# A post-norm transformer layer: first FFN layer as three fp32r products, one more FFN group ahead of the last output projection, the last group in two banks, later results on ScalarE

## The chip, the cores and the metric

One core of one Trainium2 chip runs the whole program. TensorE (PE) multiplies, VectorE (DVE), ScalarE (ACT) and GpSimd (POOL) do the elementwise work, SyncE (SP) starts the DMAs. The metric is device time in microseconds; before the change three runs took 1055.47 to 1058.67, median 1057.71.

## The reference

```python
# x: (4, 1024, 128), 16 heads of 64, all fp32
q, k, v = (einsum('BSE,EHK->BSHK', x, w) for w in (w_q, w_k, w_v))
probs = softmax(q @ k^T / sqrt(64) + causal_mask)
x = layernorm(x + einsum('BSHK,EHK->BSE', probs @ v, w_o))
h = x @ W_exp + b_exp                  # 128 -> 512
h = butterfly(h, up_weights)           # 9 linear stages
h = gelu(h + up_bias)
h = butterfly(h, down_weights)         # 9 linear stages
x = layernorm(x + h @ W_con + b_con + down_bias)
```

Both butterflies are linear, so the kernel composes them into the weights: `W1` (128 x 512) and `W2` (512 x 128). What runs over the 4096 tokens is attention, x1 = layernorm, `gelu(x1 @ W1 + b) @ W2`, and a layernorm.

## The kernel before

**Tiling.** The 4096 tokens are 32 tiles of 128 rows (`X`, batch b has 8 of them) or 8 groups of 512 (`TPC` = 4 tiles). Attention runs over 32 units, one for each batch and pair of heads. A unit has 12 steps (query chunk of 512, key tile of 128). Each step computes scores transposed, as two fp32r matmuls for each head (lines 671 and 675), exponentials on ScalarE (841), a mask (483) and a running sum of probabilities on GpSimd (498, 506, 507). `PV_AFTER` says behind which steps the value products stand (696): steps 0 to 6 of a unit behind its own steps 8 and 9, steps 7 to 11 behind step 1 of the next unit, or, for the last unit, behind everything (`PV_LEFT`).

**Order.** Every engine has its own instruction list, in an order written out by hand. `FILL`, `OUT_AT` and `X1_AT` place "fillers" for TensorE (projections 597 to 599, row maxima 621, output projection 636, transposes of x1 641, transposes of W2 645, sums 658) between the scores of a step (place 0), behind them (1) or behind the value products (2). The other engines walk the same lists (`evacuate` on ScalarE, `consume` on VectorE). Four PSUM banks `WORK` serve the fillers in turn; a filler waits until its bank's last reader is through. The score banks are `SC`, the value products' banks `O`.

**Softmax sums.** `norm` (651) multiplies the sums by ones when GpSimd's last addition of a unit is through. ScalarE writes them to `R0` (828), a DMA spreads them, VectorE takes the reciprocal (`recip`, 1027), two more DMAs copy it to all rows (`inverses`, 395), and `scale` (1032) multiplies `O` by it, after which the output projection and the next value products may use `OT` and `O`. In a unit, `recip` stands behind step 2 (`RECIP_AFTER`), `scale` behind step 6, in the last unit behind step 4 (`LAST_SCALE`).

**x1.** The first six groups (`EARLY_GROUPS`, batches 0 to 2) are normalised during later attention units, transposed by TensorE in steps 2, 3, 4, 9, 10 and 11 of the last unit, copied by VectorE into `x1T`, which lies in `WQKV` (1003), and get b_con + down_bias added in place (1015). Groups 6 and 7 follow after the last output projection: `transpose_x1` (733) and `copy_x1t` (1072).

**FFN.** `up(g)` (739) makes four hidden tiles of a group, one fp32 matmul of 128 x 512 each (746; the profile shows two instructions for each); `hid_banks` are `SC0`, `SC1` and two `WORK` banks, and a tile of group g waits for the Gelu of the same tile of group g - 1. ScalarE applies Gelu (876) into `G`, which has `DOWN_LAG` + 1 buffers. `down(g)` (749) makes the 16 products of a group (758, again two instructions each) into one of two `y_banks`. The order on TensorE is `PV_LEFT`, `norm`, `up(0)` to `up(2)`, the last output projection (636, two chunks of 16 instructions), and then `up(g)`, `down(g - 3)` in turn, with the transposes of groups 6 and 7 between, and three `down` at the end.

**End.** VectorE adds each group's product to X (`residual`: 1091, statistics 1095 and 1098), GpSimd makes (variance + eps)^-0.5 of it (`deviation`, 525: lines 528 and 531), VectorE normalises four tiles (`result`, 1100: line 1019), and SyncE stores the group (433).

Of the kernel before, what the change touches and what calls it, by code (L numbers as in the profile page):

```python
# [188 lines left out]
def post_norm_layer(nc, x, w_q, w_k, w_v, w_o, W_exp, b_exp, up_w, up_b, down_w, W_con, b_con, down_b, out):  # L189
    ctx = ExitStack()  # L190
    with ctx:
# [35 lines left out]
        RSTD = sb("RSTD", [P, B * TILES])  # L227
        HALF = sb("HALF", [P, B * TILES])
        W1 = sb("W1", [P, HID])
        SW = sb("SW", [P, 2 * HID])  # L230
# [19 lines left out]
        w2t = W2[:, :, :].rearrange("p t d -> p (t d)")  # L250
        x1T = [WQKV[:, g // 2, g % 2 * CH:(g % 2 + 1) * CH] for g in range(EARLY_GROUPS)]
        G = [w_raw[:, i * HT * CH:(i + 1) * HT * CH].rearrange("p (t c) -> p t c", t=HT) for i in range(DOWN_LAG + 1)]

# [31 lines left out]
        h1_added, stats_made = sem("h1_added"), sem("stats_made")  # L285
        x1_made, x1t_made, x1t_copied = sem("x1_made"), sem("x1t_made"), sem("x1t_copied")
        hid_ready, gelu_done, y_ready, h2_made = sem("hid_ready"), sem("gelu_done"), sem("y_ready"), sem("h2_made")
        out_made, out_stored = sem("out_made"), sem("out_stored")

# [56 lines left out]
        def _(sp):  # L346
# [83 lines left out]

            for g in range(B * CHUNKS):
                sp.wait_ge(out_made, (g + 1) * TPC)
                sp.dma_start(out_tiles[:, g * TPC:(g + 1) * TPC, :],
                             X[:, g * TPC:(g + 1) * TPC, :]).then_inc(out_stored, 16)
            sp.wait_ge(out_stored, 16 * B * CHUNKS)


        @block.gpsimd
        def _(pool):
# [108 lines left out]
            deviation((B - 1) * TILES, B * TILES)  # L548
            for g in range(B * CHUNKS):
                pool.wait_ge(x1_made, (g + 1) * TPC)  # L550
                pool.wait_ge(stats_made, (B * CHUNKS + g + 1) * TPC)
                deviation(g * TPC, (g + 1) * TPC)


        @block.tensor
        def _(pe):
# [181 lines left out]

            def up(g):
                pe.wait_ge(x1t_copied, g + 1)  # L740
                for t_ in range(HT):
                    if g == 0 and t_ >= 2:
                        evacuated(LAST_NORM - 3 + t_)
                    if g > 0:
                        pe.wait_ge(gelu_done, (g - 1) * HT + t_ + 1)
                    nc.tensor.matmul(hid_banks[t_], W1[:, t_ * P:(t_ + 1) * P], x1T[g % EARLY_GROUPS], start=True,  # L746
                                     stop=True).then_inc(hid_ready, 1)

            def down(g):
                pe.wait_ge(gelu_done, (g + 1) * HT)  # L750
                if g < 2:
                    evacuated(LAST_OUT + g)
                    evacuated(NUMBER[UNITS - 1, ("w2", 0)])
                else:
                    pe.wait_ge(h2_made, g - 1)
                for i in range(TPC):
                    for t_ in range(HT):
                        t = nc.tensor.matmul(y_banks[g % 2][:, i * P:(i + 1) * P], G[g % (DOWN_LAG + 1)][:, t_, i * P:(i + 1) * P],  # L758
                                             W2[:, t_, :], start=t_ == 0, stop=t_ == HT - 1)
                t.then_inc(y_ready, 1)  # L760

            for g in range(DOWN_LAG):
                up(g)
# [12 lines left out]
        def _(act):  # L776
# [25 lines left out]
            def evacuate(u, f, at):  # L802

                w, free = WORK[at % NWORK], work_free[at % NWORK]
                if f[0] in ("max", "mt", "out", "x1", "w2"):
                    return
                act.wait_ge(work_ready, at + 1)
                if f[0] == "proj":
                    _, n, c = f
                    nxt = (u + 1 + (f == EARLY)) % 2  # L810
                    cols = slice(c * CH, (c + 1) * CH)
                    T = QH if n == 0 else KHL
                    hi(T[0:K, nxt, 0, cols], w[0:K, :])
                    hi(T[K:P, nxt, 1, cols], w[K:P, :]).then_inc(qk_hi, 1)
                elif f[0] == "v":
                    unit, slots, tile = v_units(u)
                    if f[1] == 0 and u > 0:

                        act.wait_ge(pv_done, (u - u % 2) * NS + PV_CREDIT)
                    V = VHI if tile else VLO  # L820
                    dst = V[:, unit % slots:unit % slots + 2, 2 * f[1]:2 * f[1] + 2, :].rearrange("p u t k -> p t u k")
                    hi(dst, w[:, :].rearrange("p (t u k) -> p t u k", t=2, u=2)).then_inc(free, 1)
                elif f[0] == "lay":
                    lo = f[1] % 2 * S + f[2] * 2 * P
                    hi(XTH[:, lo:lo + 2 * P], w[:, 0:2 * P]).then_inc(xt_hi, 1)
                else:
                    act.wait_ge(sums_landed, (u - 1) * 16 + 16)
                    nc.scalar.activation(R0[:, :], w[:, :], ACT.Copy).then_inc(sums_out, 1)
                    act.wait_ge(sums_out, u)
                    act.sem_inc(free, 1)  # L830
# [40 lines left out]
            for g in range(B * CHUNKS):  # L871
                for t_ in range(HT):
                    act.wait_ge(hid_ready, g * HT + t_ + 1)
                    if t_ == 0 and g > DOWN_LAG:
                        act.wait_ge(y_ready, g - DOWN_LAG)
                    nc.scalar.activation(G[g % (DOWN_LAG + 1)][:, t_, :], hid_banks[t_], ACT.Gelu,
                                         bias=BIAS1[:, t_:t_ + 1]).then_inc(gelu_done, 1)

        @block.vector
        def _(dve):  # L880
# [54 lines left out]
            def consume(u, f, at):  # L935
# [136 lines left out]
            def copy_x1t(g):  # L1072

                dve.wait_ge(x1t_made, g - EARLY_GROUPS + 1)
                dve.wait_ge(hid_ready, (g - EARLY_GROUPS + 1) * HT)
                nc.vector.tensor_copy(x1T[g % EARLY_GROUPS], O[g % 2][:, :]).then_inc(x1t_copied, 1)
                add_bc(g)
# [8 lines left out]

            def residual(g):

                dve.wait_ge(y_ready, g + 1)
                xs = X[:, g * TPC:(g + 1) * TPC, :]  # L1090
                nc.vector.tensor_tensor(xs, y_banks[g % 2][:, :].rearrange("p (t d) -> p t d", t=TPC), xs,
                                        ALU.add).then_inc(h2_made, 1)
                dve.wait_ge(h2_made, g + 1)
                for i in range(TPC):
                    nc.vector.bn_stats(BS[:, i, :], X[:, g * TPC + i, :]).then_inc(h1_added, 1)
                dve.wait_ge(h1_added, (B * CHUNKS + g + 1) * TPC)
                for i in range(TPC):
                    nc.vector.bn_aggr(MV[:, g * TPC + i, :], BS[:, i, :]).then_inc(stats_made, 1)

            def result(g):  # L1100
                dve.wait_ge(rstd_made, B + g + 1)
                normalise(g, out_made)
# [4 lines left out]
            for g in range(B * CHUNKS):  # L1107
                residual(g)
                if g > 0:
                    result(g - 1)  # L1110
                if g + EARLY_GROUPS < B * CHUNKS:
                    copy_x1t(g + EARLY_GROUPS)
            result(B * CHUNKS - 1)


# [26 lines left out]
```

## Time and profile before

| | us |
|---|---|
| median of three runs | 1057.71 |
| profiled execution | 1057.07 |
| its span, first to last instruction | 1054.7 |
| TensorE busy | 1016.9 (96%) |
| GpSimd busy | 757.4 (72%) |
| VectorE busy | 754.2 (72%) |
| ScalarE busy | 602.9 (57%) |

The profile is of one execution of the program. Matmuls are pipelined: the duration of one holds the time until its result is out, so the pace is read from start to start. In the timelines a row is start, duration, engine, line, operation, output and inputs, count, and in brackets the idle time of the engine just before it and what ended it. In the chain of waits each piece released the next. "PEld" is TensorE's weight load, which runs beside the matmuls. The mean granted TensorE clock was 0.989 of full speed.

### The profile page before, as it was taken

How to read it: one execution, taken by the hardware profiler on the slowest of the kernel's cores; microseconds unless marked ns; L12 is line 12 of the kernel's file. 1: busy time of each engine (PE TensorE's matmuls, PEld its weight loads, DVE VectorE, ACT ScalarE, POOL GpSimd, SP SyncE). 2: the span in 40 equal slices, each digit the busy share in tenths (PEclk: the TensorE clock that was granted, in tenths of full speed). 3: DMA queues.
4: the chain of work that ended last, by engine and by line, in shares of the span. 5: the costliest groups of instructions: out<-in, count | busy, mean ns of one | idle time of the engine just before them, and what ended most of it. 6: DMA issues, size and time to landing. Idle time of an engine off the chain costs nothing.

```text
span 1054.7 us, 17699 instructions
## 1 busy us (share of the span) xinstructions
PE 1016.9 (96%) x5816; PEld 697.3 (66%) x5816; DVE 754.2 (72%) x2014; ACT 602.9 (57%) x1214; POOL 757.4 (72%) x726
## 2 busy tenths in 40 slices
PE   4799999999999999999999999999999999999997
PEld 3556666676666666767666766766666676675576
DVE  6666777777677778777778777776778778873456
ACT  4355566665565566666656556666656656664431
POOL 6278776777779777777779877777778987777322
PEclk9699999999999999999999999999999999999998
DMA  7112223232231223232231222332222222320002
GB/s 221 45 46 66 56 57 82 62 81 75 48 81 38 65 62 82 62 81 62 62 81 47 66 53 61 81 81 62 72 52 81 63 51 53 80 62 21 21 18 64
DMA packets 45800, 68.69 MB, mean 65 GB/s; under 512 B 15079, under 2 KB 21515, under 8 KB 45710
## 3 DMA queue, kind: packets, MB, share of 16 engines
q1 hardware_dynamic: 45710, 67.57, 25.2%
q8 instruction: 47, 0.77, 0.3%
q14 instruction: 43, 0.35, 0.1%
HBM read 31.11 MB, written 2.36 MB: 32 GB/s over the span
## 4 chain that ended last, share of the span: by engine, by line
PE 86%; DMA 6%; POOL 3%; DVE 2%; issue 2%; SPq 1%; ACT 0%; POOLq 0%; DVEq 0%; ACTq 0%
PE O L696 24%; PE WORK L621 13%; PE SC L671 12%; PE SC L675 12%; PE WORK L636 4%; PE WORK L658 3%; PE WORK L758 3%; PE WORK L599 3%; PE WORK L598 3%; PE WORK L597 3%; DMA QL<-NROW 2%; DMA R<-RROW 2%; PE SC L746 1%; PE WORK L746 1%; PE WORK L607 1%
## 5 line engine op out<-in xcount | busy, mean ns | idle before, releaser
L841 ACT ACTIVATE PR<-SC 128x512 f32<-128x512 f32 (+3 forms) x768 | 355.0, 490 | 283.4 <-PE SC L675 247.3
L498 POOL TENSOR_TENSOR SUM<-SUM,PR 128x1024 f32<-128x1024 f32 (+3 forms) x256 | 419.1, 1637 | 14.0
L966 DVE CUSTOM_DVE_ANT_0 WORK<-WORK,CMASK 128x128 f32<-128x128 f32 (+3 forms) x512 | 239.4, 514 | 65.0 <-PE WORK L621 65.0
L671 PE MATMUL SC<-QH,KHL 128*128 128x512 f32 (+3 forms) x768 | 272.0, 359 | 4.8 <-ACT PR L841 3.2
L675 PE MATMUL SC<-QL,KH 128*128 128x512 f32 (+3 forms) x768 | 263.9, 347 | 3.1 <-DMA QL<-NROW 3.0
L483 POOL TENSOR_SCALAR_AFFINE_SELECT PR<-PR 128x256 f32<-128x256 f32 x256 | 105.7, 414 | 213.1 <-ACT PR L841 212.9
L621 PE MATMUL WORK<-KHL,QH 128*128 128x512 f32 (+3 forms) x768 | 224.8, 361 | 5.1 <-DMA KH<-KHL 3.7
L696 PE MATMUL O<-PR,VLO 128*64 128x512 f32 (+3 forms) x1024 | 200.0, 522 | 2.0 <-DVE OT L1036 1.9
L671 PEld LDWEIGHTS SC<-QH,KHL 128*128 128x128 f32 x768 | 145.3, 189 | 63.3 <-ACT PR L841 29.2
L621 PEld LDWEIGHTS WORK<-KHL,QH 128*128 128x128 f32 x768 | 135.5, 190 | 55.8 <-issue 34.9
L969 DVE TENSOR_REDUCE MP<-WORK 128x1 f32<-128x512 f32 x256 | 164.3, 685 | 4.6
L675 PEld LDWEIGHTS SC<-QL,KH 128*128 128x128 f32 x768 | 145.5, 189 | 16.3 <-DMA QL<-NROW 5.9
L890 DVE TENSOR_TENSOR QL<-WORK,QH 64x512 fp32r<-64x512 f32 x128 | 88.1, 688 | 78.6 <-ACT QH L778 77.6
L507 POOL TENSOR_TENSOR SUM<-PR 128x768 f32<-128x768 f32 x64 | 136.3, 2130 | 1.4 <-ACT PR L841 1.4
L696 PEld LDWEIGHTS O<-PR,VLO 128*64 128x64 f32 x1024 | 64.9, 136 | 106.3 <-issue 78.4
L890 DVE TENSOR_TENSOR KHL<-WORK,KHL 64x512 fp32r<-64x512 f32 x128 | 88.1, 688 | 43.2 <-ACT KHL L778 41.1
L778 ACT ACTIVATE QH<-WORK 64x512 fp32r<-64x512 f32 x128 | 75.6, 590 | 28.6 <-PE WORK L599 27.8
L778 ACT ACTIVATE KHL<-WORK 64x512 fp32r<-64x512 f32 x128 | 75.9, 593 | 4.7 <-PE WORK L599 1.4
L696 PE MATMUL O<-PR,VHI 128*64 128x256 f32 (+3 forms) x512 | 74.3, 432 | 0.0
L966 DVE DVE_READ_ACCUMULATOR2_ANT MP<- 128x1 f32 x512 | 72.7, 142 | 0.0
L696 PEld LDWEIGHTS O<-PR,VHI 128*64 128x64 f32 x512 | 36.8, 137 | 52.6 <-issue 46.8
L636 PE MATMUL WORK<-WOT,OT 128*128 128x128 f32 x512 | 63.7, 278 | 0.0
(102 smaller groups left out, 1070.9 us busy)
## 6 DMA issues: line engine op xcount, KB each, us to landing
QH<-QH SPq DMA_DIRECT2D x128, 128.0 KB, 2.3
KH<-KHL SPq DMA_DIRECT2D x128, 128.0 KB, 2.3
R<-RROW SPq DMA_DIRECT2D x64, 256.0 KB, 3.9
SW<-in_L_ffn_up_weights_dram SPq DMA_DIRECT2D x9, 512.0 KB, 4.7
SW<-_L_ffn_down_weights_dram SPq DMA_DIRECT2D x9, 512.0 KB, 4.8
out_dram<-X SPq DMA_DIRECT2D x8, 256.0 KB, 2.3
QL<-NROW SPq DMA_DIRECT2D x64, 4.0 KB
X<-in_L_attn_x_BSE_dram SPq DMA_DIRECT2D x1, 512.0 KB, 4.3
```

Of the source, the lines that this page charges most:

```text
L498: nc.gpsimd.tensor_tensor(total, total, prob(unit, s), ALU.add).then_inc(add_done, 1)
L507: nc.gpsimd.tensor_tensor(total, first[:, :, START[s]:], prob(unit, s), ALU.add).then_inc(add_done, 1)
L621: t = nc.tensor.matmul(w[:, at_col:at_col + n], QH[:, nxt, h, qt * P:(qt + 1) * P], KHL[:, nxt, h, lo:lo + n], start=True, stop=True)
L636: t = nc.tensor.matmul(w[:, k * P:(k + 1) * P], attended(pair, qc)[:, k * P:(k + 1) * P], WOT[:, pair % PAIRS, :], start=pair < last, stop ...
L671: nc.tensor.matmul(dst, KHL[:, par, h, kt * P:(kt + 1) * P], QH[:, par, h, q0:q0 + n], start=True, stop=False)
L675: nc.tensor.matmul(dst, KH1[:, par, h, kt * P:(kt + 1) * P], QL[:, par, h, q0:q0 + n], start=False, stop=True).then_inc(scores_ready, 1)
L696: t = nc.tensor.matmul(O[qc][h * K:(h + 1) * K, START[s]:], values(unit, kt)[:, h * K:(h + 1) * K], p[:, h, :], start=kt == 0, stop=s == L ...
L778: return nc.scalar.activation(dst, src, ACT.Copy)
L841: nc.scalar.activation(prob(unit, s)[:, h, :], SC[use % NSC][:, 0:n], ACT.Exp, scale=K ** -0.5).then_inc(exp_done, 1)
L890: return nc.vector.tensor_tensor(dst, src, hi_part.bitcast(F32), ALU.subtract)
L966: op = nc.vector.tensor_tensor_reduce(cols, cols, CMASK[:, CH - n:], 1.0, LOWEST, ALU.add, ALU.max, cell)
L969: op = nc.vector.tensor_reduce(cell, cols, AX_X, ALU.max)
```

## The change

`DOWN_LAG` is 4: four groups of hidden tiles stand ahead of the last output projection, and the fifth buffer of `G` lies in `WQKV`. `W1` and x1 transposed are split into a high part, rounded to fp32r by ScalarE (`hi`), and a low part, the difference, by VectorE (`lo`); a hidden tile is three fp32r matmuls. The high parts of x1 lie in `QH` and `QL`, the low parts in `KHL` and `KH1`, the split W1 in `WST` and `WSV`, so that no group waits for another's buffer. W1 is split in step 8 of the last unit. The first two hidden tiles go ahead of the sums of the last unit. The last group is two pieces of two tiles, in two banks. Results of the first three pieces stay on VectorE, those of the other six go to ScalarE as x * rstd + shift, where GpSimd makes shift = -mean * rstd in two more operations. In the last unit `recip` and `scale` move up, to steps 1 and 3.

```diff
-DOWN_LAG = 3
+DOWN_LAG = 4
-LAST_SCALE = 4
+LAST_RECIP, LAST_SCALE = 1, 3
+FFN_PIECES = [(g * TPC, (g + 1) * TPC) for g in range(B * CHUNKS - 1)]
+FFN_PIECES += [(B * TILES - TPC, B * TILES - 2), (B * TILES - 2, B * TILES)]
+ACT_RESULTS = 3
+W1_SPLIT_AT = (UNITS - 1, 8)
...
+        def y_bank(tile):
+            return O[0] if tile >= FFN_PIECES[-1][0] else y_banks[tile // TPC % 2]
...   # SyncE: one store for each piece
+            for n, (first, end) in enumerate(FFN_PIECES):
+                if n < ACT_RESULTS:
+                    sp.wait_ge(out_made, end)
+                else:
+                    sp.wait_ge(act_out_made, end - FFN_PIECES[ACT_RESULTS][0])
+                sp.dma_start(out_tiles[:, first:end, :], X[:, first:end, :]).then_inc(out_stored, 16)
...   # GpSimd
+                deviation(first, end)
+                if n >= ACT_RESULTS:
+                    pool.wait_ge(rstd_made, B + n + 1)
+                    nc.gpsimd.tensor_tensor(SHIFT[:, first:end], MV[:, first:end, 0], RSTD[:, first:end],
+                                            ALU.mult).then_inc(shift_mult, 1)
+                    pool.wait_ge(shift_mult, n - ACT_RESULTS + 1)
+                    nc.gpsimd.tensor_scalar(SHIFT[:, first:end], SHIFT[:, first:end], -1.0, None,
+                                            ALU.mult).then_inc(shift_made, 1)
...   # TensorE
-            norm(take_work(LAST_NORM), UNITS - 1)
-            pe.wait_ge(exp_done, UNITS * 2 * NS + EXP_CREDIT)
-            def up(g):
+            def up(g, tiles=range(HT)):
                 pe.wait_ge(x1t_copied, g + 1)
-                for t_ in range(HT):
+                pe.wait_ge(w1_lo, 1)
+                for t_ in tiles:
...
-                    nc.tensor.matmul(hid_banks[t_], W1[:, t_ * P:(t_ + 1) * P], x1T[g % EARLY_GROUPS], start=True,
+                    rows = slice(t_ * P, (t_ + 1) * P)
+                    nc.tensor.matmul(hid_banks[t_], W1H[:, rows], x1_hi_slots[g], start=True, stop=False)
+                    nc.tensor.matmul(hid_banks[t_], W1L[:, rows], x1_hi_slots[g], start=False, stop=False)
+                    nc.tensor.matmul(hid_banks[t_], W1H[:, rows], x1_lo_slots[g], start=False,
                                      stop=True).then_inc(hid_ready, 1)
...
-            for g in range(DOWN_LAG):
+            pe.wait_ge(exp_done, UNITS * 2 * NS + EXP_CREDIT)
+            up(0, range(2))
+            norm(take_work(LAST_NORM), UNITS - 1)
+            up(0, range(2, HT))
+            for g in range(1, DOWN_LAG):
                 up(g)
...   # ScalarE
+                if f[0] == "x1":
+                    hi(x1_hi_slots[f[1]], w[:, :]).then_inc(x1t_hi, 1)
+                    return
...
+                    if (u, s) == W1_SPLIT_AT:
+                        act.wait_ge(composed, 3 * STAGES)
+                        hi(W1H, W1[:, :]).then_inc(w1_hi, 1)
...
+                n = g - (EARLY_GROUPS - 2)
+                if 0 <= n < B * CHUNKS - EARLY_GROUPS:
+                    act.wait_ge(x1t_made, n + 1)
+                    hi(x1_hi_slots[EARLY_GROUPS + n], O[(EARLY_GROUPS + n) % 2][:, :]).then_inc(x1t_hi, 1)
+            for n in range(ACT_RESULTS, len(FFN_PIECES)):
+                act.wait_ge(shift_made, n - ACT_RESULTS + 1)
+                for t in range(*FFN_PIECES[n]):
+                    nc.scalar.activation(X[:, t, :], X[:, t, :], ACT.Identity, scale=RSTD[:, t:t + 1],
+                                         bias=SHIFT[:, t:t + 1]).then_inc(act_out_made, 1)
...   # VectorE
-                    dve.wait_ge(work_ready, at + 1)
-                    nc.vector.tensor_copy(x1T[g], w[:, :]).then_inc(x1t_copied, 1)
+                    dve.wait_ge(x1t_hi, g + 1)
+                    lo(x1_lo_slots[g], w[:, :], x1_hi_slots[g]).then_inc(x1t_copied, 1)
...
+                    if (u, s) == W1_SPLIT_AT:
+                        dve.wait_ge(w1_hi, 1)
+                        lo(W1L, W1[:, :], W1H).then_inc(w1_lo, 1)
-                    if s == RECIP_AFTER and u > 0:
+                    if s == (RECIP_AFTER if u < UNITS - 1 else LAST_RECIP) and u > 0:
...
+            for n in range(len(FFN_PIECES)):
+                residual(n)
+                if 0 < n <= ACT_RESULTS:
+                    result(n - 1)
+                if n + EARLY_GROUPS < B * CHUNKS:
+                    copy_x1t(n + EARLY_GROUPS)
```

## Rows read from the trace of the kernel before

**Rows 1.** The page's chain that ended last, share of the span by engine

```profile
PE 86%; DMA 6%; POOL 3%; DVE 2%; issue 2%; SPq 1%; ACT 0%; POOLq 0%; DVEq 0%; ACTq 0%
```

**Rows 2.** Busy by stretch: stretch, us, PE, PEld, DVE, ACT, POOL, clock, DMA share, GB/s

```profile
962.83:985.24 22.41, 20.70 (x123) 12.41 (x122) 13.34 (x17) 8.07 (x18) 21.96 (x17) 1.00 0.09 25
985.38:1047.15 61.77, 61.76 (x368) 45.42 (x368) 29.64 (x120) 23.55 (x34) 11.45 (x16) 1.00 0.11 31
1047.15:1054.70 7.55, 0.00 (x0) 0.00 (x0) 4.06 (x17) 0.00 (x0) 1.50 (x3) 0.64 0.36 104
```

**Rows 3.** The chain in order of time, from the last sums: start, us, what

```profile
985.38 1.06 PE WORK L658 x8
...
988.35 1.72 PE WORK L746 x4
...
996.94 3.57 PE WORK L636 x32
...
1003.94 3.57 PE WORK L758 x32
```

**Rows 4.** Timeline of TensorE, two projections of unit 31 in a row

```profile
927.84 0.39 PE L597 MATMUL WORK<-XTH,WST 128*128 128x512 f32 x1
...
928.54 0.39 PE L597 MATMUL WORK<-XTH,WST 128*128 128x512 f32 x1
```

**Rows 5.** Timeline of TensorE, value products of the last unit

```profile
971.22 2.38 PE L696 MATMUL O<-PR,VLO 128*64 128x512 f32 x16 [0.95 <-DVE OT L1036]
...
982.77 2.32 PE L696 MATMUL O<-PR,VHI 128*64 128x512 f32 x16
```

**Rows 6.** Timeline of VectorE, reciprocal and scalings around the last unit

```profile
964.25 0.25 DVE L1030 RECIPROCAL RCOL<-RCOL 128x16 f32<-128x16 f32 x1
...
970.48 1.29 DVE L1036 TENSOR_TENSOR OT<-O,R 128x512 f32<-128x512 f32 x2 [1.94 <-DMA R<-RROW]
...
995.17 1.29 DVE L1036 TENSOR_TENSOR OT<-O,R 128x512 f32<-128x512 f32 x2 [5.89 <-DMA R<-RROW]
```

**Rows 7.** Timeline of ScalarE, exponentials, table load and Gelus

```profile
965.55 1.09 ACT L841 ACTIVATE PR<-SC 128x512 f32<-128x512 f32 x2 [0.34 <-PE SC L675]
...
987.20 1.28 ACT L876 ACT_TABLE_LOAD   x1
988.49 1.27 ACT L876 ACTIVATE PR<-SC,BIAS 128x512 f32<-128x512 f32 x2
...
1001.41 0.69 ACT L876 ACTIVATE PR<-SC,BIAS 128x512 f32<-128x512 f32 x1 [3.75 <-PE SC L746]
```

**Rows 8.** Timeline of VectorE and GpSimd in the last unit

```profile
976.59 0.41 POOL L483 TENSOR_SCALAR_AFFINE_SELECT PR<-PR 128x256 f32<-128x256 f32 x1
...
978.68 1.21 DVE L1015 TENSOR_TENSOR X<-X,BC 128x512 f32<-128x512 f32 x1
...
979.28 0.87 POOL L483 TENSOR_SCALAR_AFFINE_SELECT PR<-PR 128x256 f32<-128x256 f32 x1
```

**Rows 9.** The chain in order of time, last deviation

```profile
1049.35 0.37 POOL RSTD L528
```

**Rows 10.** Timeline of VectorE, the last results

```profile
1050.87 1.11 DVE L1019 TENSOR_SCALAR X<-X,MV,RSTD 128x128 f32<-128x128 f32 x4 [0.68 <-POOL RSTD L531]
```

**Rows 11.** DMA issues: count, KB each, median us from issue to landing

```profile
out_dram<-X SPq DMA_DIRECT2D x8, 256.0 KB, 2.3
```

**Rows 12.** GpSimd by form: busy us, mean ns of one, idle before

```profile
L531 POOL TENSOR_TENSOR RSTD<-RSTD,HALF 128x4 f32<-128x4 f32 x8 | 8.2, 1031 | 0.7
L531 POOL TENSOR_TENSOR RSTD<-RSTD,HALF 128x8 f32<-128x8 f32 x4 | 6.7, 1674 | 0.3
L186 POOL TENSOR_TENSOR SUM<-R,OT 4x128 f32<-4x128 f32 x14 | 6.1, 449 | 5.8 <-DMA PR<-in_L_ffn_up_weights_dram 5.3
...
L528 POOL TENSOR_SCALAR RSTD<-MV 128x8 f32<-128x8 f32 x4 | 1.0, 247 | 20.3 <-DVE MV L999 20.2
```

**Rows 13.** ScalarE by form, the smallest exponential: busy us, mean ns of one, idle

```profile
L841 ACT ACTIVATE PR<-SC 128x128 f32<-128x128 f32 x128 | 32.1, 275 | 2.6 <-PE SC L675 0.7
```

More of the change, by code:

```diff
@@ L228, in post_norm_layer @@
         HALF = sb("HALF", [P, B * TILES])
+        SHIFT = sb("SHIFT", [P, B * TILES])
         W1 = sb("W1", [P, HID])
@@ L250, in post_norm_layer @@
         w2t = W2[:, :, :].rearrange("p t d -> p (t d)")
-        x1T = [WQKV[:, g // 2, g % 2 * CH:(g % 2 + 1) * CH] for g in range(EARLY_GROUPS)]
-        G = [w_raw[:, i * HT * CH:(i + 1) * HT * CH].rearrange("p (t c) -> p t c", t=HT) for i in range(DOWN_LAG + 1)]
+        x1_hi_slots = [T[:, 0, h, c * CH:(c + 1) * CH] for T in (QH, QL) for h in range(2) for c in range(CHUNKS)]
+        x1_lo_slots = [T[:, 0, h, c * CH:(c + 1) * CH] for T in (KHL, KH1) for h in range(2) for c in range(CHUNKS)]
+        W1H = WST[:, :, :, :].rearrange("p a n c -> p (a n c)")
+        W1L = WSV[:, :, :].rearrange("p a c -> p (a c)")
+        wqkv_flat = WQKV[:, :, :].rearrange("p n c -> p (n c)")
+        G = [rows[:, i * HT * CH:(i + 1) * HT * CH].rearrange("p (t c) -> p t c", t=HT)
+             for rows, i in [(w_raw, i) for i in range(DOWN_LAG)] + [(wqkv_flat, 0)]]
         SC = [ctx.enter_context(nc.psum_tensor(f"SC{i}", [P, CH], F32)) for i in range(NSC)]
@@ L429, in _ @@
                 sp.wait_ge(dup_landed[c], 64 * UNITS)
[L431 to L435, printed above, removed]
+            for n, (first, end) in enumerate(FFN_PIECES):
[4 more added lines that the diff above has]
+                sp.dma_start(out_tiles[:, first:end, :], X[:, first:end, :]).then_inc(out_stored, 16)
+            sp.wait_ge(out_stored, 16 * len(FFN_PIECES))
         @block.gpsimd
@@ L548, in _ @@
             deviation((B - 1) * TILES, B * TILES)
[L549 to L552, printed above, removed]
+            for n, (first, end) in enumerate(FFN_PIECES):
+                pool.wait_ge(x1_made, min(end, B * TILES))
+                pool.wait_ge(stats_made, B * TILES + end)
+                deviation(first, end)
[6 more added lines that the diff above has]
+                                            ALU.mult).then_inc(shift_made, 1)
         @block.tensor
@@ L757, in down @@
                     for t_ in range(HT):
-                        t = nc.tensor.matmul(y_banks[g % 2][:, i * P:(i + 1) * P], G[g % (DOWN_LAG + 1)][:, t_, i * P:(i + 1) * P],
+                        t = nc.tensor.matmul(y_bank(g * TPC + i)[:, i * P:(i + 1) * P], G[g % (DOWN_LAG + 1)][:, t_, i * P:(i + 1) * P],
                                              W2[:, t_, :], start=t_ == 0, stop=t_ == HT - 1)
-                t.then_inc(y_ready, 1)
-            for g in range(DOWN_LAG):
+                    if any(end == g * TPC + i + 1 for _, end in FFN_PIECES):
+                        t.then_inc(y_ready, 1)
+            pe.wait_ge(exp_done, UNITS * 2 * NS + EXP_CREDIT)
[3 more added lines that the diff above has]
+            for g in range(1, DOWN_LAG):
                 up(g)
@@ L804, in evacuate @@
                 w, free = WORK[at % NWORK], work_free[at % NWORK]
-                if f[0] in ("max", "mt", "out", "x1", "w2"):
+                if f[0] in ("max", "mt", "out", "w2"):
                     return
                 act.wait_ge(work_ready, at + 1)
+                if f[0] == "x1":
+                    hi(x1_hi_slots[f[1]], w[:, :]).then_inc(x1t_hi, 1)
+                    return
                 if f[0] == "proj":
@@ L1085, in _, with residual, result @@
                 consume(UNITS + qc, ("out", qc, UNITS - 1), LAST_OUT + qc)
[L1087 to L1102, printed above, removed]
+            def residual(n):
+                first, end = FFN_PIECES[n]
+                at = first % TPC * P
+                dve.wait_ge(y_ready, n + 1)
+                xs = X[:, first:end, :]
+                y = y_bank(first)[:, at:at + (end - first) * P].rearrange("p (t d) -> p t d", t=end - first)
+                nc.vector.tensor_tensor(xs, y, xs, ALU.add).then_inc(h2_made, 1)
+                dve.wait_ge(h2_made, n + 1)
+                for t in range(first, end):
+                    nc.vector.bn_stats(BS[:, t % TPC, :], X[:, t, :]).then_inc(h1_added, 1)
+                dve.wait_ge(h1_added, B * TILES + end)
+                for t in range(first, end):
+                    nc.vector.bn_aggr(MV[:, t, :], BS[:, t % TPC, :]).then_inc(stats_made, 1)
+            def result(n):
+                dve.wait_ge(rstd_made, B + n + 1)
+                normalise(n, out_made)
             dve.wait_ge(rstd_made, B)
```

16 lines of the change are left out of this document (5 added, 11 removed).

## The prediction

> **What bounds the kernel now.** I read first the page's chain of waits, then busy time by stretch, then the chain in order of time for the last 70 us, and last the timelines of single engines there. The chain is 86% TensorE [rows 1], but the change touches three stretches with different limits. From 962.83 to 985.24 us GpSimd is busy 21.96 of 22.41 us: its additions for the last attention unit are the limit, TensorE is busy 20.70 and ScalarE only 8.07 [rows 2]. From 985.38 to 1047.15 TensorE is busy 61.76 of 61.77: it is the limit, with ScalarE at 23.55 and VectorE at 29.64 [rows 2]. Then comes a tail of 7.55 us without TensorE [rows 2]. The middle stretch holds the sums of exponentials (1.06), 32 FFN hidden tiles, the last output projection (3.57) and 8 second-layer groups of 3.57, and two transposes; two hidden tiles take 1.72, so one takes 0.86 [rows 3].
>
> **The three products.** A hidden tile was one fp32 matmul of 0.86 us. Now it is three fp32r matmuls of 128x512. The same form stands in the projections: three of them, each with its own weights, occupy TensorE from 927.84 to 928.54, 0.70 us [rows 4]; the duration column (0.39) holds the drain and is not the pace. So 0.16 us per tile less. Of 32 tiles two go ahead of the sums matmul, so behind it stand 30 x 0.70 = 21.0 instead of 32 x 0.86 = 27.5: **-6.5 us**, if nothing makes TensorE wait. Bounds of the price: 0.68 to 0.86 for three.
>
> **The two tiles ahead of the sums.** The sums matmul waited for GpSimd until 985.38. The value products of the last unit end at 982.77 + 2.32 = 985.09 [rows 5], so the gap they could fill is only 0.3 us and they need 2 x 0.70 = 1.4. What decides is whether TensorE reaches this point earlier. It stood 0.95 us at 971.22, until the scaling by the inverses [rows 5], and that scaling waited 1.94 us for the landing of R [rows 6]. Its reciprocal ran at 964.25, right behind two VectorE operations for an x1 group; moved one step up it runs some 3 us sooner, and so does the scaling, moved up as well. This wait goes. What is late next is the stream of exponentials: the x1 groups now pass ScalarE too. A 512-column copy takes about 0.6 (two exponentials of this size take 1.09), and ScalarE idles 0.34 per step there [rows 7]. Three copies stand in steps 2 to 4; they push the stream by about 0.6 (bounds 0.2 and 1.8). So the value products start 0.95 - 0.6 = 0.35 earlier, the last ones end at 984.74, the two tiles at 986.14, and the sums matmul starts there instead of 985.38: **+0.76** (bounds 0 and 1.7). The copies at steps 9 to 11 and the split of W1 come where ScalarE waits 3 us per step; GpSimd needs those exponentials only later, so I cost them at nothing; without that cover they are 0.6 each, in the rivals.
>
> The earlier scaling itself brings GpSimd nothing, since its queue is full from 962.83 on. One thing may lengthen it: X + BC on VectorE has two SBUF inputs, took 1.21 beside GpSimd's additions, and the GpSimd mask issued meanwhile took 0.87 against 0.41 otherwise [rows 8]. The new low part of W1 has two SBUF inputs too: at most 0.5 more, to 985.7, still ahead of 986.14.
> The Trainium skill, page "SBUF — State Buffer", section "SBUF: two separate sides", says that a VectorE operation with two SBUF inputs and a GpSimd operation lock each other out for a whole instruction; by it the subtraction for W1 costs GpSimd its full length, about 0.7, and the sum is still the same. The trace agrees in kind (0.87 against 0.41), not in size.
>
> **The four groups ahead of the projection.** Before, Gelu started 988.49 - 985.38 = 3.11 after the sums matmul: evacuation, then a table load of 1.28 [rows 7]. That stays in ScalarE's order, so Gelu starts at 986.14 + 3.11 = 989.25. TensorE is ready sooner: sums matmul to 987.20, tiles 3 and 4 of group 0 to 988.60; then the four banks are full and group 1 waits for the first Gelu, 989.25 + 0.69 [rows 7] and about 0.1 to signal: 990.04. **+1.44** of new idle time, before hidden by slow tiles. From there two Gelus in a row take 1.27 [rows 7], under 1.40 for two tiles, so TensorE sets the pace: 12 tiles to 998.44. The projection needs the last scaling: it started 995.17 - 985.38 = 9.79 behind the sums matmul and takes 0.65 for the first half [rows 6], so 996.6: ready 1.8 us before. Had only three groups stood there, they would end at 995.6, and it would wait about 1 us; so the fourth group covers that.
>
> **Behind the projection.** The group waits of ScalarE were 3.75 us each [rows 7]; two new copies of 0.6 fit there. VectorE's subtraction takes what its copy took; the results of six pieces leave it for ScalarE. All this at nothing; without ScalarE's cover 1.2. End of TensorE: T = 1047.15 - 6.5 + 0.76 + 1.44 = **1042.85**.
>
> **The tail.** Before, statistics reached GpSimd 1049.35 - 1047.15 = 2.20 after the last product, and the results ended at 1050.87 + 1.11 = 1051.98 [rows 9, 10], then 2.72 to the end (landing 2.3 of it [rows 11]). Now GpSimd has two more operations per piece and three pieces in the last 3.57 us. Prices: power of 4 columns 1.03, of 8 columns 1.67, so of 2 columns about 0.71; tensor_scalar 0.25; small tensor_tensor 0.45 for 128 columns [rows 12], unknown for 2 to 4. Nearest are the 0.25 and the 0.45; I take 0.25 each with 0.08 to signal: 0.66 for the shift (bounds 0.3 and 1.1 by these rows, 3.5 by the power rows). Group 6: starts T - 3.57 + 2.20 = T - 1.37, ends after 1.34 + 0.66 at T + 0.66. First half of group 7: its statistics are there, GpSimd is not: 1.05 + 0.66, to T + 2.4. Second half: statistics at about T + 1.4 (half of the VectorE work), waits for GpSimd, to T + 4.1. ScalarE: two operations of 0.275 [rows 13], T + 4.7; store 2.72: T + 7.4, against 7.55. So the tail is the same to 0.1: what the two banks save, GpSimd's queue takes back.
> Sum: 1042.85 + 7.4 = 1050.25 against 1054.70: **-4.4 us**. The profiled execution took 1057.07, 2.37 around its span: 1052.6 to 1052.7. It lies 0.64 below the median shown (1057.71), inside the spread of the runs; I forecast **1052.7**.
>
> **Rivals.**
> (a) ScalarE's seven copies (six groups, W1) do delay the exponentials, and TensorE ends the attention late. For: each exponential stands behind a copy that waits for a transpose. Against: ScalarE is busy 8.07 of 22.41. All in the way: 7 x 0.6 - 0.95 = 3.25 instead of -0.35, sums matmul at 989.7, time 1056.3; half of it 1054.5.
> (b) Three products no cheaper than one: other operands or waits per tile make it 0.86. Then -6.5 becomes -1.7 and the ScalarE wait shrinks from 1.44 to 1.1; time 1057.1. Against: 128 such triples in the projections.
> (c) GpSimd's small operations cost like its power, 1.03 to 1.67. They are six in the tail's queue; no change from 0.25 + 4.4/6 = 1.0 each, slower above; at 1.67 the time is 1061.2. For: the power is a tensor_tensor of 4 columns itself. Against: a plain one of 128 columns takes 0.45, so it is the power that is dear.
> (d) TensorE's clock falls in the new idle 1.44 us. After the last matmul the mean granted clock of 7.55 us was 0.64 [rows 2], so it does fall to 1.2 GHz in an idle stretch. At that level 12 tiles cost 8.4 more, 1061.1; it decides from 6.3 tiles at the low level. Against: through 962.83 to 985.24, with 0.95 of idle in one piece, it stayed 1.00.
> [...]
>
> **How the numbers follow.** Forecast 75%, (a) 12%, (b) 4%, (c) 5%, (d) 4%. The forecast's own range: -0.76 for the sums matmul, -1.1 for the shifts, -0.3 for the products on one side, +0.9 and +1.3 and some Gelu waits on the other: 1050.6 to 1054.6. The range of 8 in 10 takes in half of (a): 1050.6 to 1055.6. A measurement of this kernel tells 0.3%, 3.2 us, from no change: below 1054.5 counts as faster. Faster: 73 of the 75, half of (a), the mild 3 of (c), 2 of (d), 84% together; within: 2 of the forecast, the other 6 of (a) and all of (b), 12%; slower: 2 each of (c) and (d), 4%.
>
> **What would show it.** In the changed trace: hidden tiles of 0.69 to 0.70 start to start; the sums matmul near 986.1, and right ahead of it two hidden tiles; a TensorE wait for ScalarE of 1.4 us after tile 4, none after; the projection near 998.4 with no wait for VectorE; TensorE's end near 1042.9; in the tail GpSimd without idle time from T - 1.4 to T + 4.1 and the last store waiting for it. The prediction is wrong if the sums matmul comes after 988, if TensorE waits again in a later group, or if one GpSimd operation of the shift takes over 0.5 us.

## The result, and the profile after

The changed kernel took 1052.08 us (median of 12 runs, 1049.47 to 1055.26), the kernel before 1056.97 beside it (12 runs, 1054.45 to 1059.79): ratio 0.9944, 95% interval 0.9932 to 0.9956, so 0.56% or about 5.9 us faster by the ratio and 4.9 by the medians. The forecast was 1052.7 and -4.4.

The same attention part differs by several us between executions (the sums matmul of unit 30 started between 956.20 and 960.64 in the profiles of the changed kernel and of its ten variants), so I count from one event that the change doesn't touch: the start of the sums matmul of unit 30 (957.31 in the profile before, 958.42 after). From there the end came at 97.39 before and at 92.38 after: **-5.01 us**. All ends below are counted so, and so are the landmarks: each has one profiled execution behind it, while the ratios have 4 to 12 runs. Where two of these kernels do the same work up to a landmark, it repeats closely: the last sums matmul at 28.73 to 28.75 in six of them, TensorE's end at 85.16 to 85.18 in three. The end itself is read from a span given to 0.1 us, so differences of ends carry about 0.1.

Busy time by stretch after: GpSimd's work in the last unit, the stretch from the last sums matmul (it started at 987.15, the row begins 0.07 later) to TensorE's end, and the tail. The columns are those of [rows 2].

```profile
963.94:986.60 22.66, 21.97 (x128) 13.32 (x128) 17.75 (x17) 11.17 (x25) 22.22 (x17) 1.00 0.07 24
987.22:1043.58 56.36, 55.19 (x395) 49.93 (x394) 27.40 (x113) 28.96 (x48) 13.06 (x22) 1.00 0.13 36
1043.58:1050.80 7.22, 0.00 (x0) 0.00 (x0) 1.16 (x5) 3.40 (x8) 3.24 (x10) 0.85 0.33 96
```

By the landmarks (table below) the sums matmul starts 0.66 later, the stretch from it to TensorE's end is 5.32 us shorter (56.43 against 61.75), and the tail 0.35 shorter. TensorE is idle 1.17 us in a stretch where it had no gap. Its timeline shows the place, the fifth hidden tile:

```profile
989.32 0.39 PE L771 MATMUL WORK<-QH,WSV 128*128 128x512 f32 x1
989.55 0.40 PE L772 MATMUL WORK<-KHL,WST 128*128 128x512 f32 x1
991.11 0.47 PE L770 MATMUL SC<-QH,WST 128*128 128x512 f32 x1 [1.16 <-ACT PR L913]
991.42 0.39 PE L771 MATMUL SC<-QH,WSV 128*128 128x512 f32 x1
991.65 0.40 PE L772 MATMUL SC<-KHL,WST 128*128 128x512 f32 x1
991.88 0.39 PE L770 MATMUL SC<-QH,WST 128*128 128x512 f32 x1
```

Hidden tiles follow each other after 0.69 us (992.58 to 993.26 further down the timeline is 0.68), where one took 0.86 in [rows 3]. ScalarE in the same place: the evacuation, the table load, and two Gelus at a time, without a gap.

```profile
988.29 0.60 ACT L862 ACTIVATE R<-WORK 128x512 f32<-128x512 f32 x1 [5.62 <-PE WORK L683]
988.99 1.28 ACT L913 ACT_TABLE_LOAD   x1
990.28 1.27 ACT L913 ACTIVATE PR<-SC,BIAS 128x512 f32<-128x512 f32 x2
```

The 5.62 us ahead of the evacuation are what the fourth experiment uses. The tail in the chain in order of time (start, us, what), from GpSimd's work for the first half of the last group on:

```profile
1044.24 0.24 POOL RSTD L546
1044.49 0.07 issue
1044.56 0.74 POOL RSTD L549
1045.30 0.07 issue
1045.36 0.20 POOL SHIFT L573
...
1045.65 0.25 POOL SHIFT L576
1045.90 0.08 issue
1045.98 0.23 POOL RSTD L546
1046.21 0.07 issue
1046.28 0.73 POOL RSTD L549
...
1047.65 0.49 ACT X L922
```

GpSimd has no wait between its two half groups, only issue gaps of 0.07; the second half's statistics were there at 1044.84 and it began at 1045.98. The queue is the limit, as the forecast had it. The chain leaves TensorE at 1040.04 already, with the products of group 6, 3.5 us before TensorE's own end.

### The profile page after: what moved, and what is told of

Same layout as the page of the kernel before. It is cut to its first block, busy times and chain, and to the rows that moved or that the text cites. A ratio compares the mean times of both kernels' runs of the same rounds, so it can differ in the third digit from the quotient of the medians.

```text
span 1050.8 us, 17788 instructions
## 1 busy us (share of the span) xinstructions
PE 1015.5 (97%) x5848; PEld 705.9 (67%) x5848; DVE 753.7 (72%) x1996; ACT 615.1 (59%) x1243; POOL 761.3 (72%) x740
## 4 chain that ended last, share of the span: by engine, by line
PE 90%; DMA 3%; DVE 2%; POOL 2%; SPq 1%; ACT 1%; issue 1%; POOLq 0%; ACTq 0%
PE O L721 25%; PE WORK L646 14%; PE SC L696 13%; PE SC L700 13%; PE WORK L661 5%; PE WORK L683 3%; PE WORK L622 3%; PE WORK L623 3%; PE WORK L624 3%; PE WORK L784 2%; DMA QL<-NROW 2%; PE WORK L632 1%; PE WORK L634 1%; PE WORK L633 1%; POOL SUM L190 1%
## 5 line engine op out<-in xcount | busy, mean ns | idle before, releaser
L809 ACT ACTIVATE QH<-WORK 64x512 fp32r<-64x512 f32 (+1 forms) x132 | 78.0, 591 | 31.3 <-PE WORK L624 27.7
```

Of the source, the lines that this page charges most:

```text
L809: return nc.scalar.activation(dst, src, ACT.Copy)
```

## The experiments

Each is the changed kernel with one edit; "end" is counted from the sums matmul of unit 30 (kernel before 97.39, changed kernel 92.38).

| | edit | ratio to the kernel before (95%) | sums matmul | TensorE's end | end |
|---|---|---|---|---|---|
| before | | 1 | 28.07 | 89.82 | 97.39 |
| changed | | 0.9944 (0.9932 to 0.9956) | 28.73 | 85.16 | 92.38 |
| 1 | one fp32 product | 0.9995 (0.9984 to 1.0007) | 29.04 | 90.30 | 97.47 |
| 2 | sums matmul first | 0.9949 (0.9935 to 0.9964) | 28.30 | 84.73 | 91.96 |
| 3 | three groups ahead | 0.9952 (0.9936 to 0.9968) | 28.74 | 86.56 | 93.75 |
| 4 | Gelu table early | 0.9943 (0.9922 to 0.9964) | 28.73 | 83.88 | 91.12 |
| 5 | last results on VectorE | 0.9925 (0.9909 to 0.9941) | 28.75 | 85.17 | 91.10 |
| 6 | last group whole | 0.9957 (0.9943 to 0.9972) | 28.73 | 85.18 | 93.76 |
| 7 | scaling late | 0.9980 (0.9969 to 0.9991) | 31.51 | 87.94 | 95.20 |
| 8 | 4 and 2 | 0.9934 (0.9919 to 0.9949) | 28.30 | 84.50 | 91.71 |
| 9 | 4, 5, W1 split early | 0.9918 (0.9900 to 0.9937) | 28.73 | 83.85 | 89.82 |
| 10 | 2, W1 split early | 0.9941 (0.9919 to 0.9963) | 27.85 | 84.28 | 91.49 |

Against the changed kernel the ratios alone settle experiments 1 and 7, and nearly 9 (the intervals share 0.0005); for the others, where less than 1.5 us is at stake, the intervals overlap and the landmarks carry the verdict, from one execution each (the ratio of experiment 4 alone, 0.9943, shows nothing of its 1.26 us).

**1. One product.**

```diff
-                    nc.tensor.matmul(hid_banks[t_], W1H[:, rows], x1_hi_slots[g], start=True, stop=False)
-                    nc.tensor.matmul(hid_banks[t_], W1L[:, rows], x1_hi_slots[g], start=False, stop=False)
-                    nc.tensor.matmul(hid_banks[t_], W1H[:, rows], x1_lo_slots[g], start=False,
+                    nc.tensor.matmul(hid_banks[t_], W1[:, rows], x1_hi_slots[g].bitcast(F32), start=True,
```

> The changed kernel with each hidden tile made by one fp32 matmul (W1 times the high part of x1) in place of the three fp32r ones; the low part of x1 is left out of the result, all copies and subtractions stay. My theory: the three products are the gain. A tile goes from 0.69 to 0.86 us start to start, 30 of them behind the sums matmul and 2 ahead: +0.17 x 32 = 5.4, less about 0.2 to 0.5 of the wait for the first Gelu, so +5 us against the changed kernel: about 1057, ratio to the kernel before 0.999 to 1.000. Rival: the gain came from the reordering and the tail, and the products are worth little: ratio stays under 0.997. In the profile: hidden tiles 0.86 apart, the end of TensorE 5 us later counted from the sums matmul of unit 30.

The end went to 97.47, +5.09. TensorE's timeline shows two tiles in 1.72 us (994.92 to 996.64), so 0.86 for one:

```profile
993.13 1.96 PE L770 MATMUL SC<-QH,W 128*128 128x512 f32 x4 [0.98 <-ACT PR L911]
994.92 1.88 PE L770 MATMUL WORK<-QH,W 128*128 128x512 f32 x4
996.64 1.88 PE L770 MATMUL SC<-QH,W 128*128 128x512 f32 x4
```

All the rest of the change together is worth nothing in this form (0.9995). But the copies and subtractions that make the high and low parts are still in this kernel, and they cost time of their own. What the new order and the new tail would give without any splitting, with the plain fp32 products of before, was not run.

**2. Sums matmul first.**

```diff
-            up(0, range(2))
             norm(take_work(LAST_NORM), UNITS - 1)
-            up(0, range(2, HT))
+            up(0)
```

> The changed kernel with the last sums matmul ahead of all hidden tiles, as before. My theory: everything from the fifth hidden tile on hangs on the first Gelu, and that on the sums matmul, so the two tiles ahead of it cost what they delay it: GpSimd ends 0.6 us before the sums matmul starts now (986.60 against 987.22). The sums matmul then starts 0.5 us earlier, the four tiles behind it end about when the first Gelu does, the wait of TensorE for ScalarE goes from 1.2 to about 0, and TensorE ends 0.5 us earlier: -0.5 us against the changed kernel, about 1051.6. Rival: the two tiles fill time that was idle, so without them TensorE ends later by up to 2 x 0.69 = 1.4 us: 1053.5.

-0.42. The wait for Gelu is gone, and TensorE waits 1.08 us ahead of the sums matmul instead:

```profile
985.54 2.32 PE L721 MATMUL O<-PR,VHI 128*64 128x512 f32 x16
988.94 1.07 PE L683 MATMUL WORK<-SUM,ONES 128*32 128x512 f32 x8 [1.08 <-POOL SUM L516]
989.94 0.50 PE L770 MATMUL SC<-QH,WST 128*128 128x512 f32 x1
```

Start to start the gap is 1.15 (985.54 to 988.94, of which the value products need 2.25). The two tiles did fill it, but they overran it by 0.43, and what they won was handed to the wait for Gelu. Part of the change was a small loss.

**3. Three groups ahead.** `DOWN_LAG = 3`.

> The changed kernel with three groups of hidden tiles ahead of the last output projection, as before. My theory: the last scaling is ready 0.65 us into 996.96, that is 997.6; three groups end at 991.11 + 8 x 0.70 = 996.7, so TensorE waits about 0.9 us for it and ends 0.9 later: +0.9 against the changed kernel, about 1053.0. Rival A: with the fourth group away the projection simply comes earlier and nothing is lost: +0. Rival B: the group also paid for later waits (Gelu before its products): +2 or more, with waits of TensorE for ScalarE in later groups.

+1.37, and the wait is where it was expected, 1.12 against my 0.9, with none in later groups:

```profile
996.88 0.39 PE L772 MATMUL WORK<-KHL,WST 128*128 128x512 f32 x1
998.39 1.80 PE L661 MATMUL WORK<-WOT,OT 128*128 128x128 f32 x14 [1.12 <-DVE OT L1082]
```

The start to start distance (998.39 - 996.88 = 1.51, where 0.23 is the pace) gives 1.3 of loss; the bracket leaves out the drain of the matmul before.

**4. Gelu table early.**

```diff
+        WARM = sb("WARM", [P, 1])
...   # ScalarE
+            nc.scalar.activation(WARM[:, :], ONES[:, 0:1], ACT.Gelu)
             evacuate(UNITS, ("norm", 1), LAST_NORM)
```

> The changed kernel with one Gelu on a column of ones, result unused, in ScalarE's list ahead of the evacuation of the last sums, so that the table load of 1.28 us runs while ScalarE is idle. My theory: the first Gelu then starts 1.3 us earlier after the sums matmul (about 1.75 instead of 3.06), before the banks are full, and the 1.16 to 1.3 us in which TensorE waits for it go: -1.3 us against the changed kernel, about 1050.8; the projection then starts about 10.7 after the sums matmul and the scaling is ready at about 10.4, so no new wait. Rival A: the evacuation uses Copy and loads a table of its own again, so that two more loads come: 0 or +1.3. Rival B: the wait only moves to the scaling by the inverses, which comes 9.7 + 0.65 after the sums matmul: -0.8 or less, with a wait of TensorE for VectorE ahead of the projection.

-1.26. The first Gelu starts 1.85 after the sums matmul instead of 3.13, no TensorE wait is left, and the copy between is not followed by a second load (ScalarE's timeline):

```profile
984.35 1.28 ACT L907 ACT_TABLE_LOAD   x1
985.64 0.20 ACT L907 ACTIVATE WARM<-ONES 128x1 f32<-128x1 f32 x1
989.94 0.60 ACT L863 ACTIVATE R<-WORK 128x512 f32<-128x512 f32 x1 [4.10 <-PE WORK L684]
990.66 1.27 ACT L915 ACTIVATE PR<-SC,BIAS 128x512 f32<-128x512 f32 x2
```

**5. Last results on VectorE.** Pieces 7 and 8 (two tiles each).

```diff
+DVE_AGAIN = B * CHUNKS - 1
...   # SyncE: the stores of these pieces wait for VectorE
+                elif n >= DVE_AGAIN:
+                    sp.wait_ge(out_made, ACT_RESULTS * TPC + end - FFN_PIECES[DVE_AGAIN][0])
...   # GpSimd: shift
-                if n >= ACT_RESULTS:
+                if ACT_RESULTS <= n < DVE_AGAIN:
...   # ScalarE: results
-            for n in range(ACT_RESULTS, len(FFN_PIECES)):
+            for n in range(ACT_RESULTS, DVE_AGAIN):
...   # VectorE, at its end
+            for n in range(DVE_AGAIN, len(FFN_PIECES)):
+                dve.wait_ge(rstd_made, B + n + 1)
+                for t in range(*FFN_PIECES[n]):
+                    normalise_tile(t, out_made)
```

> The changed kernel with the results of the last two pieces (two tiles each) on VectorE again, so that GpSimd makes no shift for them; pieces 3 to 6 stay on ScalarE. My theory: after TensorE's end the tail is GpSimd's queue (seven operations from 1044.24 to 1047.61) and then ScalarE. Without the four shift operations it ends 0.6 + 0.6 us earlier, at 1046.4, and VectorE's two tiles take 0.6 where ScalarE's took 0.9: tail 7.22 becomes about 5.9, -1.3 us against the changed kernel, about 1050.8. Rival: the last group's statistics on VectorE set the tail (they end at 1044.84), not GpSimd: then -0.3 at most, the difference of the last two tiles alone.

-1.28, tail 5.93. GpSimd goes from one power straight to the next piece, and VectorE's two tiles take 0.60 where ScalarE's took 0.88 (timeline, rows of GpSimd and VectorE). Only the last two pieces were moved back; whether pieces 3 to 6 gain anything from ScalarE was not tested.

```profile
1042.03 0.23 POOL L549 TENSOR_SCALAR RSTD<-MV 128x2 f32<-128x2 f32 x1
1042.34 0.72 POOL L552 TENSOR_TENSOR RSTD<-RSTD,HALF 128x2 f32<-128x2 f32 x1
...
1043.08 0.22 POOL L549 TENSOR_SCALAR RSTD<-MV 128x2 f32<-128x2 f32 x1
...
1043.39 0.71 POOL L552 TENSOR_TENSOR RSTD<-RSTD,HALF 128x2 f32<-128x2 f32 x1
1044.14 0.60 DVE L1068 TENSOR_SCALAR X<-X,MV,RSTD 128x128 f32<-128x128 f32 x2 [0.43 <-POOL RSTD L552]
```

**6. Last group whole.** `FFN_PIECES = [(g * TPC, (g + 1) * TPC) for g in range(B * CHUNKS)]`.

> The changed kernel with the last group in one piece and one bank, its four results on ScalarE. My theory: GpSimd gets the statistics 2.1 us after TensorE's end, needs 2.0, ScalarE 1.65 for four tiles, the store 2.3: tail 8.0 against 7.22, +0.8 us, about 1052.9. Rival: the halves win nothing, since their GpSimd operations queue (3.4 us for both): tail within 0.2 of 7.22.

+1.38, more than the 0.8 expected: ScalarE ended 5.8 us after TensorE, as reckoned, but the store of 256 KB then took 2.75 us to the end, that of half the size 2.27.

**7. Scaling late.** `LAST_RECIP, LAST_SCALE = 2, 4`.

> The changed kernel with the reciprocal and the scaling of the last unit back behind steps 2 and 4. My theory: the reciprocal then stands behind the first x1 group on VectorE (which now ends at 967.04, 8.6 after the sums matmul of unit 30, since its X + BC waits for GpSimd), R lands 6.2 later, the value products start about 2.5 us later than now, and all behind them is limited by TensorE: +2.5 us, about 1054.6. Rival: GpSimd limits the last unit anyway (busy 22.22 of 22.66), so the sums matmul moves by less than 0.5: about 1052.3.

+2.82. The reciprocal came behind the first x1 group, 8.66 after the sums matmul of unit 30 (before 6.94, changed kernel 3.64), and TensorE waited 2.72, [rows 5] had 0.95. VectorE's timeline:

```profile
966.50 0.69 DVE L936 TENSOR_TENSOR KHL<-WORK,QH 128x512 fp32r<-128x512 f32 x1 [7.93 <-ACT QH L809]
967.34 1.78 DVE L1061 TENSOR_TENSOR X<-X,BC 128x512 f32<-128x512 f32 x1
969.16 0.25 DVE L1076 RECIPROCAL RCOL<-RCOL 128x16 f32<-128x16 f32 x1
...
972.07 2.61 DVE L1061 TENSOR_TENSOR X<-X,BC 128x512 f32<-128x512 f32 x1
975.62 1.29 DVE L1082 TENSOR_TENSOR OT<-O,R 128x512 f32<-128x512 f32 x2 [0.93 <-DMA R<-RROW]
```

The 2.61 us of the third X + BC cost nothing here: the scaling waited another 0.93 for R. What is on the path is the first group. Its subtraction waits for ScalarE's copy and starts 0.63 later than the copy of before did, its X + BC takes 1.09 us longer, and the DMAs 0.23; together that is 1.95 more than before (value products at 15.86 against 13.91).

**8. Table early and sums first.** Edits 4 and 2.

> The changed kernel with the Gelu table loaded early (as in the fourth experiment) and the last sums matmul ahead of all hidden tiles (as in the second). My theory: with the wait for Gelu gone, all behind the sums matmul is TensorE work, so the two tiles ahead of it are worth their 1.38 less the 0.43 by which they delay it: this kernel is 0.95 slower than the fourth alone, though the same edit made 0.42 of gain on the changed kernel; counted from the sums matmul of unit 30 the end is at 92.1, against 91.1 for the fourth and 92.4 for the changed kernel. Rival: the two gains add up (end at 90.7), since the sums matmul is the start of the last chain in either case.

91.71: 0.59 worse than experiment 4, where the same edit gained 0.42 on the changed kernel. The sign turned, as expected. The size is short by 0.36: in experiment 4 the projection starts 10.95 after the sums matmul where 1.06 + 14 x 0.69 gives 10.7, so some 0.25 is lost there. TensorE's timelines show where: in experiment 4 the three tiles behind the sums matmul take 0.83, 0.85 and 0.78 from start to start, in experiment 8 the first takes 0.80 and the rest 0.68 to 0.69. What slows them is not shown.

**9. Three gains.** Edits 4 and 5, and `W1_SPLIT_AT = (UNITS - 1, 1)`.

> The changed kernel with the Gelu table loaded early, the last two pieces' results on VectorE, and W1 split behind step 1 of the last unit instead of step 8. My theory: the first saves 1.26 in front of TensorE's end and the second 1.28 behind it, so they add up; the third saves nothing here, since TensorE and not GpSimd is last ahead of the sums matmul. Counted from the sums matmul of unit 30 the end comes at 89.8 (changed kernel 92.4, kernel before 97.4); ratio to the kernel before 0.992, about 1049.5 where the kernel before has 1057. Rival: the gains overlap or a new wait for the scaling or GpSimd's queue takes one back: end at 90.5 or later.

89.82, -2.56 on the changed kernel and -7.57 on the kernel before: the two savings (1.26 and 1.28) add up, within the 0.1 to which an end is known. The median was 1049.72 beside 1058.02 for the kernel before. This is the fastest version by its end and by its ratio, though the ratio's interval overlaps those of experiments 5, 8 and others. GpSimd's end came earlier (27.71 against 28.18) and the sums matmul did not move: it is TensorE that is last there.

**10. W1 split early, sums first.** Edit 2 and `W1_SPLIT_AT = (UNITS - 1, 1)`.

> The second experiment (sums matmul first) with W1 split behind step 1 of the last unit instead of step 8. There GpSimd's last addition and not TensorE holds the sums matmul. My theory: at step 8 the subtraction for W1 (two SBUF inputs) costs GpSimd 0.7 us, seen as an addition of 2.64 instead of 2.37 and a mask of 0.86 instead of 0.41; behind step 1 GpSimd is idle, so its end comes at 27.45 instead of 28.16 after the sums matmul of unit 30, the sums matmul at 27.6 instead of 28.3 and the end at 91.3 instead of 91.96. Rival: the longer rows are an artefact of the profile, or another VectorE operation takes the place: GpSimd's end stays within 0.2 of 28.16.

GpSimd's end came at 27.70, 0.46 earlier, and the end 0.47 earlier than in experiment 2. Half of my reading fell: the long addition stays (2.65), so it isn't the subtraction's doing; the mask behind it is back at 0.40. GpSimd's timeline of this experiment, and then of the changed kernel at the same place:

```profile
973.29 2.65 POOL L516 TENSOR_TENSOR SUM<-SUM,PR 128x1024 f32<-128x1024 f32 x1
975.90 0.40 POOL L501 TENSOR_SCALAR_AFFINE_SELECT PR<-PR 128x256 f32<-128x256 f32 x1
```

```profile
972.21 2.64 POOL L516 TENSOR_TENSOR SUM<-SUM,PR 128x1024 f32<-128x1024 f32 x1
974.80 0.86 POOL L501 TENSOR_SCALAR_AFFINE_SELECT PR<-PR 128x256 f32<-128x256 f32 x1
```

So one VectorE operation with two SBUF inputs costs GpSimd 0.46 here, what the forecast had read off the two masks of [rows 8]. The traces also say what lengthens the addition: another such operation, X + BC of the third x1 group, still runs when it starts. In the changed kernel that is until 972.61, 0.40 into the addition, in experiment 10 until 973.70, 0.41 into it. VectorE's timeline of the changed kernel:

```profile
971.18 1.43 DVE L1061 TENSOR_TENSOR X<-X,BC 128x512 f32<-128x512 f32 x1
972.65 2.75 DVE L936 TENSOR_TENSOR WSV<-W,WST 128x512 fp32r<-128x512 f32 x1
```

In experiments 2, 7, 8 and 9 the overlap is 0.39 to 0.41 as well and the addition takes 2.62 to 2.64; before the change no operation with two SBUF inputs overlapped it, and it took 2.37. No experiment moved this X + BC alone.

## Why the prediction was right, and where it was off

| step | forecast | measured |
|---|---|---|
| hidden tile | 0.70 | 0.69 |
| sums matmul, from that of unit 30 | 28.83 | 28.73 |
| first Gelu behind it | 3.11 | 3.13 |
| TensorE's wait at the fifth tile | 1.44 | 1.3 start to start |
| last projection | 41.13 | 40.96 |
| TensorE's end | 85.54 | 85.16 |
| GpSimd's last shift, from TensorE's end (T) | 4.1 | 4.03 |
| ScalarE's last result, from T | 4.7 | 4.95 |
| tail | 7.4 | 7.22 |

**The products** carry the gain. The -6.5 of the forecast has two parts: 32 tiles that are 0.16 shorter, 5.1, and two tiles of 0.70 that moved ahead of the sums, 1.4. Experiment 1 takes back the first part alone and cost 5.09: 32 tiles that are 0.17 longer, 5.4 (0.31 of it ahead of the sums matmul, at 29.04), less what the slower tiles hide of the Gelu wait (0.98 in place of 1.16) and a remainder under 0.2 that is not placed. The pace read from the projections [rows 4] held; rival (b) is out.

The experiments price each piece against the finished kernel: 5.09, 2.82 for the moved scaling, 1.37 for the fourth group, 0.10 for the new tail (1.38 less 1.28) and -0.42 for the two tiles make 8.96, not 5.01. The pieces depend on each other. The copies and subtractions make the scaling's path longer, for one, and what the splitting costs as a whole was not measured.

**The agreement of the times** is in part luck. The forecast of 1052.7 is 0.6 from the median, but twelve executions of the same kernel spread over 5.8 us, and the ratio gives -5.9 where the medians give -4.9. The landmarks are the sharper test: TensorE's end 0.38 earlier than forecast and the tail 0.18 shorter. The forecast's own range was also added up slightly short, since 1052.7 + 0.9 + 1.3 is 1054.9 and not 1054.6.

**The two tiles ahead of the sums.** 28.83 against 28.73 hides two misses of opposite sign. I let the three copies push the exponentials by 0.6; the value products started 13.07 after the sums matmul of unit 30 where the position before, less its wait, was 12.96, so the push was 0.1. But the copies at steps 9 to 11, costed at nothing, held TensorE for about 0.26 ahead of the last scores (0.65 from the transposes to them, 0.39 before), and the two tiles took 1.59 from the last value product to the sums matmul, not 1.40. Rival (a) is out: the copies cost 0.1 and 0.26 of the 4.2 that it had for them. What the forecast left unsaid is that these two tiles were a loss: it had the +0.76 and the +1.44 side by side and didn't ask what the order before would give. It gives -0.42.

**VectorE against GpSimd.** The forecast took the mask's 0.87 against 0.41 [rows 8] as too little for an operation of 1.21 us that holds it off for its whole length. The same trace explains the size: X + BC, started at 978.68, had itself stood until GpSimd's addition ended at 979.34, ran 0.55 more, and only that part fell on the mask (last section).

**The moved scaling** was priced by the old wait of 0.95. Its worth in the changed kernel is 2.82, because ScalarE's copy and the longer X + BC of the first x1 group made the path that it left longer (experiment 7). The sum came out right, since it needed only that the wait was gone.

**The fourth group** was costed as cover for a wait of about 1 us; 1.37 measured.

**The tail.** "What the two banks save, GpSimd's queue takes back" was right as a sum (7.22 against 7.57). Its parts: with the last group whole, the shifts and ScalarE make the tail 8.58, 1.01 more than before, and the halves then save 1.36 (experiment 6). Taking the shifts and ScalarE out of the last two pieces gives 1.28 (experiment 5). The small GpSimd operations cost 0.20 and 0.25, as taken; rival (c) is out. Two terms were off and cancelled: ScalarE needs 0.88 for two tiles (479 ns each), not the 0.55 of the exponentials in [rows 13], and the store of half the size is 0.45 quicker than the 2.72 taken.

**The clock** stayed at 1.00 of 2.4 GHz through the 1.2 us wait of the changed kernel (first row), and in experiment 7 through one of 2.7 us, here with the stretch behind it; rival (d) did not occur.

```profile
989.60:991.20 1.60, 0.44 (x3) 0.12 (x2) 0.25 (x1) 1.59 (x3) 0.00 (x0) 1.00 0.04 5
973.60:976.40 2.80, 0.08 (x3) 0.04 (x2) 1.87 (x3) 1.19 (x3) 2.66 (x2) 1.00 0.25 57
976.40:980.00 3.60, 3.60 (x22) 1.86 (x24) 1.10 (x2) 0.68 (x2) 3.60 (x3) 1.00 0.00 0
```

That doesn't make a wait of 2.7 us safe everywhere. The forecast looked at the tail alone for a fall, but the page of the kernel before shows one in the second of its 40 slices of 26.4 us, where TensorE works in short bursts (tenths of full speed):

```profile
PEclk9699999999999999999999999999999999999998
```

There the clock is 0.50, so 1.2 GHz, from 36 to 44 us, around and behind a wait of 2.27 us that ends at 37.35; in the 2 us from 34 on TensorE had been busy 1.04. Ahead of the wait of experiment 7 it had been busy 4.94 of 5.60 us. Why one wait has the lower clock behind it and the other has not is not shown.

## What to carry to other kernels

When work is moved ahead of the instruction that starts the last chain, compare the gap it fills with its length: 1.15 of gap (start to start) and 1.59 of work cost 0.43 at the start of that chain, and the same move was worth +0.59 as soon as the chain's next wait, a table load that an idle ScalarE could have done 5 us before, was gone. A second pass over the end of a kernel should count the small operations in the slowest queue: four GpSimd operations of 0.2 to 0.25 with their issue gaps, and ScalarE in VectorE's place, were all that stood against the gain of two banks. And price a moved step by the path that it would stand in after the change, not by the wait that the old trace shows.

## What the hardware showed that I had not expected

- VectorE's subtraction of two SBUF operands took 2.75 us beside GpSimd's additions and 0.69 ahead of them (experiment 10, split behind step 1). Where such an operation overlaps one of GpSimd in these traces, the one that started later pays. The subtraction ended 0.55 us after the addition that it had found running (975.40 against 974.85; in experiment 2 977.62 against 977.07), and the mask behind it took 0.86 in place of 0.40. It also goes the other way: GpSimd's addition of 768 columns took 2.37 where X + BC had started 0.02 ahead of it (kernel before, at 963.54), and 1.81 where nothing was ahead of it (at 980.13). VectorE pays more often here because it mostly comes second, behind additions of 2.4 us.
- The same result costs more on ScalarE: two 128x128 tiles as Identity with scale and bias take 0.88 us (479 ns each, start to start about 0.4), as one VectorE operation each 0.60.
- A ScalarE that shows busy all the time need not be the limit. In the stretch of the hidden tiles of the changed kernel it is busy 8.30 of 8.30 us, as is TensorE (columns as in [rows 2]):

```profile
991.20:999.50 8.30, 8.30 (x38) 6.87 (x39) 1.29 (x2) 8.30 (x14) 0.00 (x0) 1.00 0.23 64
```

  But its first Gelus, with tiles waiting, start 0.58 apart (990.28 and, two later, 991.44), the later ones 0.68, TensorE's pace; the durations of 0.69 overlap.
